# Gated cross-attention with a top-2 expert layer: column parts for the experts' weights, exp from the score PSUM, and an earlier first layer norm

## The reference

```python
q = LN(x) @ Wq + bq ; k = ctx @ Wk + bk ; v = ctx @ Wv + bv        # head dim 32
s = (q @ k.T) / sqrt(512)
s = (s - mean(s)) / (std(s, ddof=1) + 1e-8)                        # over the 722 keys
s = s + where(mask, -1e-32, 0) ; attn = softmax(s)
x = x + tanh(g_xattn) * (tile(attn @ v, 16) @ Wout + bout)         # the head repeated 16 times
n = LN(x) ; probs = softmax(n @ router_w.T) ; w, idx = top_k(probs, 2) ; w = w / (sum(w) + 1e-6)
y_e = (silu(n @ gate_e) * (n @ up_e)) @ w2_e                       # w13: 512 x 2048, w2: 1024 x 512
x = x + tanh(g_ffn) * sum over the two chosen experts of w * y_e
```

## Time and profile before

| what | us |
|---|---|
| median of 3 runs | 531.41 |
| their range | 523.58 to 532.26 |
| the profiled execution | 529.5 |
| its span, first to last instruction | 527.9 |
| TensorE busy, share of the span | 422.1 (80%) |
| mean granted TensorE clock, as a share of 2.4 GHz | 0.858 |

### The profile page before, as it was taken

The page is one execution under the profiler, slowest core; times in us unless marked ns, Lnnn a source line. Parts: engine busy times, 40 slices in busy tenths (PEclk is TensorE's granted clock), DMA queues, the critical chain, the costliest instruction groups (busy, mean ns, idle before and its releaser), DMA issues.

```text
span 527.9 us, 7587 instructions
## 1 busy us (share of the span) xinstructions
PE 422.1 (80%) x2108; PEld 307.7 (58%) x2109; DVE 243.1 (46%) x491; ACT 195.6 (37%) x319; POOL 194.9 (37%) x340
## 2 busy tenths in 40 slices
PE   3668986888662129999994099999999999999991
PEld 1234554445441127778773078777877877787781
DVE  0245663445545131475571454138537557367220
ACT  0032331232424211473560552237447266265220
POOL 2433475676657421234343003220413434235121
PEclk9796895766755559999998579999999999999997
DMA  7554665449210007626816706901492671880021
GB/s 220 174 185 159 192 201 130 151 152 353 76 34 13 0 21 264 236 40 199 321 34 230 279 0 214 333 23 23 130 368 42 222 291 30 285 265 21 5 40 13
DMA packets 25795, 78.78 MB, mean 149 GB/s; under 512 B 6041, under 2 KB 6049, under 8 KB 20658
## 3 DMA queue, kind: packets, MB, share of 16 engines
q1 hardware_dynamic: 19266, 67.51, 35.4%
q0 software_dynamic: 4752, 7.80, 8.2%
q10 hardware_dynamic: 1760, 3.28, 2.0%
HBM read 71.92 MB, written 7.57 MB: 151 GB/s over the span
## 4 chain that ended last, share of the span: by engine, by line
PE 61%; POOL 11%; DMA 9%; issue 8%; DVE 4%; SPq 2%; ACT 1%; POOLq 1%; DVEq 0%; ACTq 0%
PE scp L476 16%; PE turnA L456 16%; PE turnB L456 15%; PE kvp L463 2%; PE kvp L410 2%; DMA stage<-in_L_ffn_w_dram 2%; PE kvp L332 2%; POOL lists_d L969 2%; DMA ent_next<-lists_d 2%; DMA xg<-xn_d,gidx 2%; PE scp L442 1%; PE turnA L425 1%; POOL hot L998 1%; DMA g_in<-in_g_ffn_dram 1%; POOL rs L921 1%
## 5 line engine op out<-in xcount | busy, mean ns | idle before, releaser
L691 DVE TENSOR_TENSOR w13l<-stage,w13h 128x1024 fp32r<-128x1024 f32 x64 | 76.4, 1219 | 26.2 <-ACT w13h L537 25.8
L537 ACT ACTIVATE w13h<-stage 128x1024 fp32r<-128x1024 f32 x64 | 64.7, 1052 | 22.5 <-DMA stage<-in_L_ffn_w_dram 22.5
L476 PE MATMUL scp<-w2h,hTh 128*128 128x512 f32 x128 | 56.8, 444 | 2.3 <-DVE hTl L862 2.3
L456 PE MATMUL turnA<-w13h,xTh 128*128 128x512 f32 x128 | 53.2, 416 | 4.8 <-DVE xTl L851 4.8
L456 PE MATMUL turnB<-w13h,xTh 128*128 128x512 f32 x128 | 51.9, 406 | 0.0
L476 PE MATMUL scp<-w2l,hTh 128*128 128x512 f32 x128 | 51.6, 403 | 0.0
L456 PE MATMUL turnA<-w13l,xTh 128*128 128x512 f32 x128 | 51.5, 403 | 0.0
L456 PE MATMUL turnA<-w13h,xTl 128*128 128x512 f32 x128 | 51.5, 403 | 0.0
L476 PE MATMUL scp<-w2h,hTl 128*128 128x512 f32 x128 | 51.2, 400 | 0.0
L456 PE MATMUL turnB<-w13h,xTl 128*128 128x512 f32 x128 | 50.6, 395 | 0.0
L456 PE MATMUL turnB<-w13l,xTh 128*128 128x512 f32 x128 | 50.5, 395 | 0.0
(11 more groups left out here) (167 smaller groups left out, 737.2 us busy)
## 6 DMA issues: line engine op xcount, KB each, us to landing
stage<-in_L_ffn_w_dram SPq DMA_DIRECT2D x48, 1024.0 KB, 11.8
ctx_t<-in_ctx_dram SPq DMA_DIRECT2D x8, 1444.0 KB, 7.3
mterm<-mterm_d SPq DMA_DIRECT2D x8, 282.0 KB
x_t<-in_x_dram SPq DMA_DIRECT2D x8, 200.0 KB
out_dram<-x ACTq DMA_DIRECT2D x8, 200.0 KB
xn_d<-xn ACTq DMA_DIRECT2D x8, 200.0 KB
ctx_t<-in_L_xattn_Wout_dram SPq DMA_DIRECT2D x1, 1024.0 KB, 7.1
ent_next<-lists_d POOLq DMA_DIRECT2D x17, 1.0 KB, 2.0
```

What stands on the lines that cost most here:

```text
L456: mm = pe.matmul(region, xp[:, c, :], rhs, start=(c == 0 and i == 0), stop=(c == HC - 1 and i == 2))
L476: mm = pe.matmul(scp[:, 512:512 + H], hp[:, q, j * P:(j + 1) * P], wp[:, q * QC + j, :], start=(q == 0 and j == 0 and i == 0), stop=(q == ...
L537: act.activation(dst, src, ACT.Copy).then_inc(S["w_hi"], 1)
L691: dve.tensor_tensor(lo, raw, hi.bitcast(F32), ALU.subtract).then_inc(S["w_lo"], 1)
```

## The change

**Weights.** The host lays w13 out as 8 experts x 4 column quarters x 128 partitions x 2048, and w2 as two halves in the same manner, so that each 1 MB transfer brings one quarter q of gate and up for all 512 rows, 8 KB contiguous per partition. `stage13`, `w13h` and `w13l` are `[P, NQ, HC, 2 * QW]`. SP loads quarter q of expert e as soon as units 2q and 2q+1 of expert e-1 are split; the wait for a gather is kept once, ahead of the loop. ScalarE waits for a quarter only ahead of its own first unit.

**Scores.** The mask becomes a factor on v: `emask` = exp(mask term), with keys on partitions; VectorE multiplies it into `vn` instead of copying, and GpSimd writes it as a 65th column of `vn`, so that the head product's row 65 is the softmax sum. Exp reads the score PSUM directly, with sigma's scale and bias and no maximum taken off. A one-column product (`pick_sum`) brings the sum to one value per token in PSUM. The maximum, the mask loads, `z` and `psum_p` are gone. The constant row is now row 65 of `wsum`, so the output product adds it; `xc` and `residual` are gone, and VectorE adds x itself (x is four deep).

**Order.** `norm1` on GpSimd moves from behind the one-hot steps to right behind `rstd2`, and `ln1_stats` on VectorE to right behind the q copy. The reciprocal of the sum moves to ahead of x2.

```diff
+        stage13 = sb(es, "stage13", [P, NQ, HC, 2 * QW])
+        w13h = sb(es, "w13h", [P, NQ, HC, 2 * QW], F32R)
+        w13l = sb(es, "w13l", [P, NQ, HC, 2 * QW], F32R)
...
+                if b >= 4:
+                    sp.wait_ge(S["x2_ready"], b - 3)
+                elif b == 2:
+                    sp.wait_ge(S["crow_done"], 1)
+                elif b == 3:
+                    sp.wait_ge(S["rw_turned"], 1)
+                sp.dma_start(x_t[b % 4][:], x[b]).then_inc(S[f"x_in{b % 4}"], 16)
...
             sp.wait_ge(S["attn_done"], 4)
+            sp.wait_ge(S["gathered"], 16)
             with sp.Fori(1, E) as e:
-                sp.wait_ge(S["w_lo"], e * W_UNITS - 2)
-                before = sp.value_load(first_tile[0:1, bass.ds(e - 1, 1)], min_val=0, max_val=TILES - 1)
-                sp.wait_ge(S["gathered"], before * 16 + 32)
-                for c in range(HC):
-                    sp.dma_start(stage13[:, c, :], w13[bass.ds(e, 1), c * P:(c + 1) * P, :].rearrange("o p n -> p (o n)")
-                                 ).then_inc(S[f"st13_{c}"], 16)
+                for q in range(NQ):
+                    sp.wait_ge(S["w_lo"], e * W_UNITS - W_UNITS + 2 * q + 2)
+                    sp.dma_start(stage13[:, q, :, :], w13[bass.ds(e, 1), q].rearrange("o p (c n) -> p (o c) n", c=HC)
+                                 ).then_inc(S[f"st13_{q}"], 16)
                 for u in range(2):
                     sp.wait_ge(S["w_lo"], e * W_UNITS - 1 + u)
-                    hic = IC // 2
-                    sp.dma_start(stage2[:, u * hic:(u + 1) * hic, :],
-                                 w2[bass.ds(e, 1), u * hic * P:(u + 1) * hic * P, :].rearrange("o (c p) n -> p (o c) n", p=P)
+                    sp.dma_start(stage2[:, u * IC // 2:(u + 1) * IC // 2, :],
+                                 w2[bass.ds(e, 1), u].rearrange("o p (c n) -> p (o c) n", n=H)
                                  ).then_inc(S[f"st2_{u}"], 16)
...
+            pe.matmul(scp[2 * D:2 * D + 1, 0:H], bv_c[:], wsum[0:D, :], start=True, stop=False)
+            pe.matmul(scp[2 * D:2 * D + 1, 0:H], ones[0:1, 0:1], bout_r, start=False, stop=True).then_inc(S["crow_done"], 1)
...
+                    pe.wait_ge(S["vsum_set"], b + 1)
                     for k in range(KT):
                         n = P if k < KT - 1 else KL
-                        mm = pe.matmul(kvp[0:2 * D, 0:SQ], vn[b % 2][0:n, k, :], probT[0:n, k, :], start=(k == 0), stop=(k == KT - 1))
+                        mm = pe.matmul(kvp[0:2 * D + 1, 0:SQ], vn[b % 2][0:n, k, :], probT[0:n, k, :], start=(k == 0), stop=(k == KT - 1))
                     mm.then_inc(S["head_done"], 1)
...
+                    if b == 0:
+                        pe.wait_ge(S["pick_made"], 2)
+                    pe.matmul(turnB[0:SQ, 640:641], headT[:], pick_sum[:], start=True, stop=True).then_inc(S["sum_done"], 1)
                     if live(i):
                         pe.wait_ge(S["v_copied"], 2 * (i + 1))
                     pe.matmul(turnA[0:SQ, 0:H], headT[:], wsum[:], start=True, stop=True).then_inc(S["out_done"], 1)
...
-                        rhs = wp[:, c, :].rearrange("p (g n) -> p g n", g=2)[:, :, q * QW:(q + 1) * QW]
-                        mm = pe.matmul(region, xp[:, c, :], rhs, start=(c == 0 and i == 0), stop=(c == HC - 1 and i == 2))
+                        mm = pe.matmul(region, xp[:, c, :], wp[:, q, c, :], start=(c == 0 and i == 0), stop=(c == HC - 1 and i == 2))
...
+            act.wait_ge(S["mask_made"], 1)
+            act.activation(emask[:].rearrange("p b k -> p (b k)"), mask_f[:], ACT.Exp).then_inc(S["emask_made"], 1)
...
-                act.wait_ge(S["negmax"], b + 1)
-                if b >= 1:
                     act.wait_ge(S["prob_turned"], b)
-                    act.wait_ge(S["gsum"], b)
-                act.activation(prob[:], z[:], ACT.Exp, bias=zmax[:, 1:2], accum_out=psum_p[:]).then_inc(S["exp_done"], 1)
+                act.activation(prob[:], scp[0:SQ, 0:SK], ACT.Exp, bias=sig[:, 5:6], scale=sig[:, 3:4]).then_inc(S["exp_done"], 1)
...
-                if unit == 0:
-                    for c in range(HC):
-                        act.wait_ge(S[f"st13_{c}"], e * 16 + 16)
+                if unit < 2 * NQ and unit % 2 == 0:
+                    act.wait_ge(S[f"st13_{unit // 2}"], e * 16 + 16)
...
                                       ).then_inc(S["q_copied"], 1)
+                if live(i + 1) and i >= 0:
+                    ln1_stats(i + 1)
...
-                    dve.wait_ge(S["z_done"], b + 1)
-                    dve.wait_ge(S[f"mterm_in{b % 2}"], 16 * (b // 2 + 1))
-                    if b >= 1:
-                        dve.wait_ge(S["exp_done"], b)
-                    dve.tensor_tensor_reduce(out=z[:], in0=z[:], in1=mterm[b % 2][:], scale=1.0, scalar=-3.0e38,
-                                             op0=ALU.add, op1=ALU.max, accum_out=zmax[:, 0:1]).then_inc(S["z_masked"], 1)
-                    dve.wait_ge(S["z_masked"], b + 1)
-                    dve.tensor_scalar(zmax[:, 1:2], zmax[:, 0:1], -1.0, None, ALU.mult).then_inc(S["negmax"], 1)
...
-                    ln1_stats(i + 1)
...
-                    dve.reciprocal(gs[:, 0:1], psum_p[:]).then_inc(S["rsum"], 1)
-                    dve.wait_ge(S["rsum"], b + 1)
-                    dve.tensor_scalar(gs[:, 1:2], gs[:, 0:1], g_t[0:SQ, 0:1], None, ALU.mult).then_inc(S["gsum"], 1)
...
+                    dve.tensor_tensor(vn[i % 2][:, 0:KT - 1, 0:2 * D],
+                                      turnA[:, 0:(KT - 1) * 2 * D].rearrange("p (k d) -> p k d", d=2 * D),
+                                      emask[:, i, 0:KT - 1].unsqueeze(2).to_broadcast([P, KT - 1, 2 * D]), ALU.mult
+                                      ).then_inc(S["v_copied"], 1)
+                    dve.tensor_scalar(vn[i % 2][0:KL, KT - 1, 0:2 * D], turnA[0:KL, (KT - 1) * 2 * D:KT * 2 * D],
+                                      emask[0:KL, i, KT - 1:KT], None, ALU.mult).then_inc(S["v_copied"], 1)
...
+                    dve.wait_ge(S["sum_done"], b + 1)
+                    if b >= 1:
+                        dve.wait_ge(S["x2_ready"], b)
+                    else:
+                        dve.wait_ge(S["tanh_done"], 1)
+                    dve.reciprocal(gs[:, 0:1], turnB[0:SQ, 640:641]).then_inc(S["sum_inv"], 1)
+                    dve.wait_ge(S["sum_inv"], b + 1)
+                    dve.tensor_scalar(gs[:, 1:2], gs[:, 0:1], g_t[0:SQ, 0:1], None, ALU.mult).then_inc(S["gsum"], 1)
...
-                    dve.wait_ge(S["xc_ready"], b + 1)
                     if b >= 2:
                         dve.wait_ge(S[f"out_put{b % 2}"], 16 * (b // 2))
                         dve.wait_ge(S["xn2_ready"], b - 1)
-                    dve.scalar_tensor_tensor(out=x2[b % 2][:], in0=turnA[0:SQ, 0:H], scalar=gs[:, 1:2], in1=xc[b % 3][:],
+                    dve.scalar_tensor_tensor(out=x2[b % 2][:], in0=turnA[0:SQ, 0:H], scalar=gs[:, 1:2], in1=x_t[b % 4][:],
...
             for i in ROUNDS:
+                if live(i):
+                    if i == 0:
+                        pool.wait_ge(S["emask_made"], 1)
+                    if i >= 2:
+                        pool.wait_ge(S["head_done"], i - 1)
+                    pool.tensor_copy(vn[i % 2][:, :, 2 * D:2 * D + 1], emask[:, i, :].unsqueeze(2)).then_inc(S["vsum_set"], 1)
                 if live(i - 2):
                     b = i - 2
                     pool.wait_ge(S["ln2_aggr"], b + 1)
                     if b >= 1:
                         pool.wait_ge(S["xn2_ready"], b)
                     rstd(ln2[b % 2], rs2, "rstd2")
+                if live(i + 1) and i >= 0:
+                    norm1(i + 1)
...
-                if live(i + 1) and i >= 0:
-                    residual(i + 1)
...
-                if live(i + 1) and i >= 0:
-                    norm1(i + 1)
...
+        if name == "L0_ffn_w13":
+            a = _np.ascontiguousarray(a.reshape(8, 4, 128, 2, 4, 256).transpose(0, 4, 2, 1, 3, 5)).reshape(8, 4, 128, 2048)
+            arrays[f"in_{name}_dram"] = a
+        if name == "L0_ffn_w2":
+            a = _np.ascontiguousarray(a.reshape(8, 2, 4, 128, 512).transpose(0, 1, 3, 2, 4)).reshape(8, 2, 128, 2048)
```

139 lines of the change are left out of this document (44 added, 95 removed).

## The result

The changed kernel takes 482.19 us (median of 4 runs, 480.62 to 485.01) beside 531.84 for the kernel before (523.58 to 534.01). The sign and both large terms had the right cause; the term for the four attention rounds was too small by 10 us.

What follows compares the result with a forecast made beforehand. TensorE was taken to set steady tiles, with time lost to a weight stall in the single-tile expert and waits in attention. Savings of 23.0 + 6.7 + 2.2 + 1.5 = 33.4 from 529.5 gave 496 us, range 485 to 508.

Steps and rivals of the forecast that it cites:

- both large terms: The two largest savings summed: the single-tile expert's weight stall, minus 23.0 us, and the four attention rounds, minus 6.7.
- the term for the four attention rounds: Four rounds between heads from 67.77 to 135.11: 67.3 us becomes 60.6, minus 6.7 us.
- Column parts: Single-tile expert: weights in column parts land in time, no stall, tile costs 18.5 instead of 41.5 us, minus 23.0.
- Waits before the heads: Attention: TensorE's waits for probT of 3.87, 1.48 and 1.53 us go, with layer norm ahead of routing.
- What is late next is TensorE itself, 15.6 us: Attention rounds without the waits: TensorE sets 15.6 us a round, read from the round from 119.5; one high-clock round excepted.
- The rival that the clock stays up: Attention rounds all run like the one at clock 0.93, GpSimd's 13.2 us sets four rounds; 484 us, chance 0.15.
- GpSimd's floor: GpSimd's list of a round falls from 13.9 to 13.0 us: residual add gone, 128x6 copy added at 0.4.
- Earlier rounds: Attention before the four rounds: waits of 2.04 and 0.61 us go, 0.4 added for two sums, minus 2.2.
- Tail: End of attention: the last batch's probT loses the mask step and an idle 0.77 us; minus 1.5 with the sum.
- Only the stall goes: Rival: only the single tile's 23.0 us is won, attention's rounds give nothing; 506.5 us, chance 0.14.
- Parts land late: Rival: each weight part meets the 16.7 us landing and gates the next, half the stall stays; 507.5 us, chance 0.07.
- Slower: Rival: in seven reloads, weights run over GpSimd's fetch, gather and row add, delaying y; 534.5 us, chance 0.02.

Runs made afterwards that it cites:

- loads_together: Changed kernel, but SP issues all four parts of an expert only once all the previous expert's w13 units are split; 480.96 us, ratio 0.9067.
- early_norm_only: Kernel before with only `ln1_stats` and `norm1` moved ahead of routing, as the change moves them; 513.18 us, ratio 0.9728.
- head_waits: Changed kernel with head products of rounds 4 to 7 made to wait for GpSimd's weight step of the same round; 493.92 us, ratio 0.9330.
- exp_only: Kernel before with exp straight from the score PSUM, without z, the maximum and the mask term; mask loads stay; 519.43 us, ratio 0.9771.
- weights_only: Kernel before with only the column parts (weight layout, SP's loop by parts, ScalarE's wait per part); 505.42 us, ratio 0.9629.
- no_gather_wait: Kernel before without SP's wait for a gather, row parts and unit 0's wait for all four kept; 520.46 us, ratio 0.9896.
- before_filled: Kernel before with eight throw-away 128x128 products ahead of the head product's wait for probT in rounds 3 to 7; 529.78 us, ratio 0.9947.
- tail_best: Changed kernel with 36 throw-away products before the first tile and VectorE's first-expert splits moved out of GpSimd's way; 473.20 us, ratio 0.8978.

## Why the prediction was right on the weights and too small on attention

**Column parts: minus 23.0 forecast, minus 21.1 measured.** Right. The parts come in time: line 508 never waits for one. And the parts are worth nothing in steady tiles. The tile takes 20.2 us instead of 18.5, because this one tile must split w2 of its own expert and all of w13 of the next, and I took it for an ordinary tile (TensorE waits 1.07 us in it for VectorE's `hTl`, which stands among these splits); that these splits make up the whole 1.7 us is argued. The other 0.2 is scatter. My reason was half right: I let the gain hang on the issue "some 3 us apart", and loads_together shows that issuing the first part about 10 us later costs nothing here once SP's gather wait (14.1 us) and unit 0's wait for all parts (7 us) are gone.

**Waits before the heads: they go.** Right: the releasers, the rounds and the move were read right, and early_norm_only confirms it by itself.

**"What is late next is TensorE itself, 15.6 us": the step that failed.** The rounds' term was minus 6.7 and measured minus 17.2. I took the round from 119.5 in the earlier trace rows as what TensorE needs by itself. It is what it needs at a mean clock of 0.67. With the waits gone three of four rounds in the kernel after ran at clock 1.00, with 10.3 us of products in each, and in two of them, of 11.7 and 11.8 us, GpSimd's list is full. The four rounds measured 50.2 where the sum had 60.6, which is 10.4 of the 14 us by which the forecast was too high. head_waits shows the mechanism in the other direction, and early_norm_only shows part of it in the kernel before (0.72 to 0.79). What spoke against it in my text (94% busy and yet 0.67) was a wrong argument: three rounds of nearly the same products in the same order ran at 1.00, with TensorE busy for 82 to 88% of them, so a busy share of 94% goes with the low clock and is no sign that the clock stays low at full work. The low level didn't vanish: the round from 85.90 has no wait before its head, is busy 13.20 of 14.10 us, and ran at 0.76. The rival that the clock stays up gave 484 us, with a chance of 0.15, and it is the one that came nearest; three of its four rounds happened, each shorter than the 13.2 us that it gave them.

**GpSimd's floor: 13.0 forecast, 11.8 measured.** The copy of 128x6 took 0.20 us, not 0.4. The other 1.1 us are three small steps that were longer in the kernel before: `nlmax` 0.50 us instead of 0.24, the cast of `place` 0.84 instead of 0.19, a step of `wgt` 0.41 instead of 0.22. The longest lay under VectorE's masked maximum, which is gone now. GpSimd's and VectorE's timelines before, then GpSimd's after:

```profile
74.48 0.84 POOL L962 CAST place<-place_f 100x2 int32<-100x2 f32 x1
```

```profile
74.38 0.90 DVE L728 CUSTOM_DVE_ANT_0 z<-z,mterm 100x722 f32<-100x722 f32 x1
```

```profile
81.61 0.19 POOL L914 CAST place<-place_f 100x2 int32<-100x2 f32 x1
```

**Earlier rounds: minus 2.2 forecast.** The wait of 2.04 us went whole, but the first head came only 1.0 us sooner, since the projection ahead of it ran longer at the lower clock (4.67 us against 3.52). The next two rounds gained 4.0 and 0.4: 14.3 us to 10.3, and 13.3 to 12.9. From the first head to the third: 27.6 before, 23.2 now. Minus 5.4 in all, again more than the waits; exp_only, with exp alone changed, has 6.9 of it there.

**Tail: minus 1.5 forecast.** From the seventh head to the eighth 12.6 became 10.4, and the rest of the tail moved by 0.3: minus 2.5. The sum of attention's three measured parts, 5.4 + 17.2 + 2.5, is 25.1 of the 25.2.

**The other rivals.** *Only the stall goes* would have been 506.5; weights_only measured 505.4, so its number was right for that half alone. *Parts land late* had no sign: the longest landing is 7.9 us, and nothing waits for one. *Slower*, by GpSimd's transfers: the waits for `ent_next` sum to 48.5 us over 17 fetches (48.2 before), GpSimd still has 99.4 us of idle time ahead of its fetches, and steady tiles kept 18.5 us. The steady tiles have the room, as the prediction argued. The effect itself exists: in no_gather_wait, where the loads run ahead of the first gather and nothing hides it, it costs 5.4 us.

**What stays open.** What holds the clock at the lower level in rounds that have no wait before the head (one of four in the kernel after, three of four in early_norm_only); whether a cheaper filling than before_filled's would leave a gain; how much the norm's place is worth beside the rest of the change; and why attention in tail_best's profile is 5 us shorter than its edits explain.

## What to carry to other kernels

Where TensorE's busy time is long at a granted clock under 1, don't take that time as its floor: work out the round at either level, and ask whether the waits that the change removes are part of what holds it at the lower one. Splitting a transfer pays through the consumer's wait per part; look first for the wait that ends last (here a gather that the transfer never needed, but keep such a wait where it holds bulk loads behind a small transfer that everything waits for). And a bulk VectorE step laid beside small GpSimd steps on the path costs those steps about 2 us each, so place it where GpSimd has nothing that others wait for.

## What the runs showed of the hardware that I had not expected

Waits of 0.56 to 1.57 us before a head product, 4.1 us in four rounds, went with a granted clock of 0.78 instead of 0.87 to 0.93, and 5.8 to 9.1 us more of busy time for the same 377 products. A 100x8 GpSimd step of 0.20 us took 2.43 under two 128x1024 splits on VectorE. Four 1 MB loads issued within about 2 us were all there 13.0 us later (no_gather_wait), and the first within 5.5 (loads_together). With the weights' loads running over GpSimd's fetches, gathers and row adds, its waits for the lists changed by 0.3 us in 48.
